# Own halves of the circular and of the last convolution ahead of the waits for their halo rows, and twelve unread matmuls between the halves of the last image

## The chip, the cores and the metric

The kernel runs on one core of one Trainium2 chip. The metric is the device time of one execution in microseconds (us), as the median of several runs; lower is better.

## What is computed

The input `x` is a batch of 8 images of 16 channels and 64 x 64 pixels in f32. Four blocks follow each other, each of them `x = x + conv(group_norm(x))`:

```python
x = x + _L0_conv_ref(_gn(x), L0_conv_W, L0_conv_b)      # a 4 x 4 lattice of 3x3 convolutions
x = x + _L1_conv_ref(_gn(x), L1_conv_weight)            # a circular 3x3 convolution
x = x + _L2_conv_ref(_gn(x), L2_conv_base_weight, L2_conv_spline_weight, L2_conv_spline_scaler, L2_conv_bias_weight)
x = x + _L3_conv_ref(_gn(x), L3_conv_combinator, L3_conv_bias)   # a 3x3 convolution with bias
```

`_gn` normalises each image over 8 groups of 2 channels and all pixels. The second block is written in the reference with FFTs and amounts to a 3x3 convolution with circular borders. The third expands each pixel into 8 spline functions and a SiLU and convolves these 9 features. The fourth is a plain 3x3 convolution with zero borders plus a bias.

## The kernel before, in words

Each engine has a program of its own, written out by hand in the order in which it runs; semaphores (`wait_ge`, `then_inc`) tie the programs together. An engine runs its instructions strictly in that order, so a wait holds up everything behind it. PE is TensorE, DVE VectorE, ACT ScalarE, POOL GpSimd, SP the engine that issues most transfers.

An f32 operand is split into a high and a low part (ACT writes the high part, DVE subtracts it and writes the low one), and each f32 product is three matmuls (`PRODUCTS`, in `products`, L1741 at the matmul): high by high, high by low, low by high. Pixels lie in SBUF with 128 rows: 4 rows of the image by 2 column parities by 16 channels. An output row at the edge of such a group of four needs rows of a neighbouring group. These are the halo rows: SP copies them with four transfers from the tile of own rows to a second tile, once the low part is written.

- The lattice (L1772) runs as 16 cells by 8 images. In its last cell, `k == NC - 1`, PE also runs the circular convolution of image `b - 4` after cell image `b` (`l1_step`). Images 4 to 7 of the circular convolution follow when the cells are over: `l1_step(B - 4)`, `l1_step(B - 3)`, the 2-column matmul `group_means(1, 3)` for the statistics of the next block (L1679), 24 unread matmuls (`keep_warm`, L1809), `l1_step(B - 2)`, `group_means(1, 4)`, 4 unread matmuls, `l1_step(B - 1)`.
- `l1_step(j)` waits for `l1_lo` (DVE has written the low part, L1495), for `l1_halo` (four transfers of SP, L805, `l1_halos`), and for `added[1]` (DVE has read the result bank of image `j - 2`, L1500), and then runs 12 matmuls in `single_step`: 6 on the own tile `F1_OWN`, 6 on the halo tile `F1_HALO`, all into one bank.
- The third block is called KAN here. Its features come from a chain of DVE (L1596, L1602, L1609, L1589) and ACT (L1216, L1227, L1230, L1243) in two groups per image; per image PE runs 24 matmuls for group 0, the halo steps of the image before, 6 for the SiLU, 12 for `l3_step(b - 3)` and 24 for group 1.
- `l3_step(b)`, the last convolution, waits for `l3_lo` (DVE L1566), `l3_halo` (four transfers of SP, L844, `l3_halos`) and `out_staged` (DVE has emptied the bank of image `b - 2`, L1577), and runs `single_step` on 12 matmuls. Images 0 to 4 lie inside the loop; behind the loop stand `group_means(2, 6)`, the halo steps of image 7, `l3_step(5)`, `group_means(2, 7)`, `l3_step(6)`, `l3_step(7)`.
- Behind each `l3_step` DVE adds bias and residual into `OT` (`last_update`, L1577, two instructions) and `OT` is stored with four transfers: for images 5 to 7 two by POOL (L1111) and two by SP (L869). Before `last_update(7)` writes its half of `OT`, it waits for the stores of image 5 on both queues. SP's program has `l3_halos(7)` ahead of the stores of images 5, 6 and 7.

Of the kernel before, what the change touches and what calls it, by code (L numbers as in the profile page):

```python
# [11 lines left out]
B = 8  # L12
# [39 lines left out]
SLOTS_1 = 3  # L52
# [106 lines left out]
def build(nc, x, l0w, l0b, l1w, l2base, l2spline, l2scale, l2bias, l3w, l3bias, consts, out):  # L159
# [80 lines left out]
    with ctx:  # L240
        def sb(name, shape, dt=F32):
            return ctx.enter_context(nc.sbuf_tensor(name, shape, dt))

        def sem(name):
            return ctx.enter_context(nc.semaphore(name))
# [6 lines left out]
        W3 = sb("W3", [P, 2, 4, P], F32R)  # L252
# [35 lines left out]
        W1 = WX[:, 0:8 * P].rearrange("p (a t m) -> p a t m", a=2, m=P)  # L288
# [9 lines left out]
        F1_OWN, F1_HALO = F1[:, :, :, RW:RW + TS], F1[:, :, :, EXT:EXT + TS]  # L298
# [19 lines left out]
        def wide(a):  # L318

            return a.rearrange("p (y w) -> p y w", w=RW)  # L320

        def pixels(a):

            return a.rearrange("p (y w) -> p y w", w=RX)
# [13 lines left out]
        def l3_slot(b):  # L338

            return L3S[max(0, b - B + 3)]  # L340

        PB = [ctx.enter_context(nc.psum_tensor(f"PB{i}", [P, 512], F32)) for i in range(8)]
        OUT_BANK = PB[0:2]
        SPLINE_BANK = (PB[5], PB[6], PB[0])
        RING_BANK = PB[3:7]
        LAST_BANK = PB[3:5]
# [54 lines left out]
        l1_ns, l1_hi, l1_lo, l1_done = sem("l1_ns"), sem("l1_hi"), sem("l1_lo"), sem("l1_done")  # L401
        l1_halo = [sem(f"l1_halo{z}") for z in range(SLOTS_1)]
        l3_ns, l3_hi, l3_lo, l3_done = sem("l3_ns"), sem("l3_hi"), sem("l3_lo"), sem("l3_done")
        l3_halo = [sem(f"l3_halo{z}") for z in range(3)]
# [1264 lines left out]
        def _(pe):  # L1669
# [67 lines left out]
            def products(bank, todo, open_, close):  # L1737

                todo = [(weights[wp], moving[fp]) for weights, moving in todo for wp, fp in PRODUCTS]
                for n, (weights, moving) in enumerate(todo):  # L1740
                    last = nc.tensor.matmul(pixels(bank[:, :]), weights, moving,  # L1741
                                            start=open_ and n == 0, stop=close and n == len(todo) - 1)
                return last

            def at_shift(tile, rows, dx):

                return [wide(tile[0:rows, part])[:, :, dx:dx + RX] for part in range(2)]
# [26 lines left out]
                                                    start=j == 0, stop=j == len(todo) - 1)  # L1774
                        last.then_inc(out_done, 1)

            def single_step(bank, weights, own, halo):

                todo = [((weights[:, 0, 1 - dx], weights[:, 1, 1 - dx]), at_shift(own, P, dx)) for dx in range(2)]
                products(bank, todo, True, False)  # L1780
                todo = [((weights[:, 0, 3 - dx], weights[:, 1, 3 - dx]), at_shift(halo, P, dx))
                        for dx in range(2)]
                return products(bank, todo, False, True)

            def l1_step(j):

                z = j % SLOTS_1
                pe.wait_ge(l1_lo, j + 1)
                pe.wait_ge(l1_halo[z], 4 * 16 * (j // SLOTS_1 + 1))
                if j >= 2:  # L1790
                    pe.wait_ge(added[1], j - 1)
                single_step(OUT_BANK[j % 2], W1, F1_OWN[:, z], F1_HALO[:, z]).then_inc(l1_done, 1)

            turn("cell0")
            pe.wait_ge(mv_ready, 1)
# [10 lines left out]
            def keep_warm(bank, n):  # L1806

                for i in range(n):
                    nc.tensor.matmul(bank[:, :], W3[:, 0, 0], W3[:, 0].rearrange("p t m -> p (t m)"),  # L1809
                                     start=True, stop=True)  # L1810

            keep_warm(PB[2], 8)
            for s in range(STEPS):
                k, b = divmod(s, B)
                if b == 0 and k in (1, 5):
                    keep_warm(PB[2], 10 if k == 1 else 18)
                cell_step(s)
                if (k, b) in TURN_STEPS:
                    turn(TURN_STEPS[k, b])
                if k == NC - 1:  # L1820
                    if b == 0:
                        pe.wait_ge(w1_loaded, dma_total(single_spread(W1)))
                        pe.wait_ge(bias_ready, 1)
                    if b >= 1:
                        group_means(0, b - 1)
                    if b >= 5:
                        group_means(1, b - 5)
                    if b == 4:
                        keep_warm(PB[1], 10)
                    if b >= 4:  # L1830
                        l1_step(b - 4)
            group_means(0, B - 1)
            l1_step(B - 4)
            pe.wait_ge(evac_done, TOTCH)
            pe.wait_ge(w3_loaded, dma_total(single_spread(W3)))
            l1_step(B - 3)
            group_means(1, 3)
            keep_warm(PB[3], 24)
# [18 lines left out]
            def l3_step(b):  # L1857

                z = max(0, b - B + 3)
                pe.wait_ge(l3_lo, b + 1)  # L1860
                pe.wait_ge(l3_halo[z], 4 * 16 * (b + 1 if z == 0 else 1))
                if b >= 2:
                    pe.wait_ge(out_staged, b - 1)
                single_step(LAST_BANK[b % 2], W3, l3_slot(b)[:, 0], l3_slot(b)[:, 1]).then_inc(l3_done, 1)

            def halo_steps(b, g):

# [9 lines left out]
            for b in range(B):  # L1877
                bank = SPLINE_BANK[b % 3]
# [6 lines left out]
                for g in range(KAN_SETS):  # L1885
                    pe.wait_ge(feat_hi, KAN_SETS * b + g + 1)
                    pe.wait_ge(feat_lo, KAN_SETS * b + g + 1)
                    todo = [(own_weights(t, dx), at_shift(feature(t), P, dx))
                            for t in range(GROUP * g, GROUP * (g + 1)) for dx in range(2)]
                    products(bank, todo, g == 0, False).then_inc(tile_used, 1)  # L1890
                    if g == 0:
                        if b < 2:
                            group_means(1, (5, 7)[b])
                        if b == 1:
                            pe.wait_ge(edge_done, 2)
                        if b:
                            halo_steps(b - 1, 0)
                            halo_steps(b - 1, 1)
                        pe.wait_ge(silu_hi, b + 1)
                        pe.wait_ge(silu_lo, b + 1)  # L1900
                        todo = [(own_weights(BASES, dx), at_shift(feature(BASES), P, dx)) for dx in range(2)]
                        products(bank, todo, False, False).then_inc(tile_used, 1)
                        if b >= 3:
                            l3_step(b - 3)
# [4 lines left out]
            halo_steps(B - 1, 0)  # L1909
            halo_steps(B - 1, 1)  # L1910
            l3_step(B - 3)
            group_means(2, B - 1)
            l3_step(B - 2)
            l3_step(B - 1)

# [58 lines left out]
```

## Time and profile before

| | |
|---|---|
| median of 3 runs | 1261.64 us |
| the three runs | 1259.15, 1261.64, 1265.6 us |
| the profiled execution's own time | 1263.95 us |
| its span, first to last instruction | 1262.1 us |
| PE busy | 1177.1 us (93%) |
| DVE busy | 762.3 us (60%) |
| ACT busy | 676.3 us (54%) |
| mean granted TensorE clock | 0.982 |

The profiled execution is a fourth one. Its own time is 1.85 us above its span. Busy time is summed over the whole span; what an engine holds up has to be read from the stretch in question. The granted clock is the share of full speed that TensorE was given: 1.00 is 2.4 GHz, 0.50 is 1.2 GHz.

### The profile page before, as it was taken

To read this page: it belongs to the slowest core of one execution; us is meant where nothing else is said; L and a number is where in the kernel's file an instruction comes from. 1 tells how busy PE (TensorE), PEld (TensorE's weight loads), DVE (VectorE), ACT (ScalarE), POOL (GpSimd) and SP (SyncE) were. 2 spreads that over 40 slices of the span, in tenths; PEclk is the share of its full clock that TensorE was granted. 3 is DMA by queue.
4 is the path that set the end of the run, shared out by engine and by line. 5 is a ranking of instruction groups with operands and counts; after the bars stand their busy time and mean duration, and the time that the engine had idled before them with its cause. 6 is when DMAs were issued, how large, how long until landed. Compare 5 with 4: busy or idle time off the path is not lost.

```text
span 1262.1 us, 14781 instructions
## 1 busy us (share of the span) xinstructions
PE 1177.1 (93%) x5052; PEld 871.8 (69%) x5052; DVE 762.3 (60%) x967; ACT 676.3 (54%) x737; POOL 379.3 (30%) x553
## 2 busy tenths in 40 slices
PE   2988989989999999989999999998999987999995
PEld 1655667666666677766666677777777766777773
DVE  6898962456555522245655552236655789899952
ACT  2677854345445434445445444344444799789821
POOL 8231333424422012412122303634134442104212
PEclk9999999999999999999999999999999998999998
DMA  6899999999999968999999988978799414777873
GB/s 172 230 249 243 289 265 248 183 173 209 209 194 198 218 187 217 218 185 206 201 210 202 197 213 213 256 204 224 193 206 196 59 32 69 108 115 108 126 124 58
DMA packets 103342, 233.65 MB, mean 185 GB/s; under 512 B 35476, under 2 KB 48356, under 8 KB 94884
## 3 DMA queue, kind: packets, MB, share of 16 engines
q1 hardware_dynamic: 80768, 179.28, 65.6%
q0 software_dynamic: 16064, 24.70, 10.8%
q10 hardware_dynamic: 6436, 28.74, 7.3%
q8 instruction: 40, 0.66, 0.2%
q14 instruction: 34, 0.28, 0.1%
HBM read 123.59 MB, written 85.19 MB: 165 GB/s over the span
## 4 chain that ended last, share of the span: by engine, by line
PE 56%; SPq 17%; DVE 12%; DMA 5%; issue 5%; ACT 3%; POOL 2%; DVEq 0%; ACTq 0%; POOLq 0%
PE PB L1772 48%; SPq L830 14%; PE PB L1741 7%; DMA S<-lattice 2%; DVE F L1472 2%; DVE F L1484 2%; DMA F<-F 2%; DVE S L1609 1%; DVE S L1596 1%; DVE S L1602 1%; ACT F L1167 1%; DVE F L1589 1%; SPq L812 1%; SPq L861 1%; ACT F L1243 1%
## 5 line engine op out<-in xcount | busy, mean ns | idle before, releaser
L1772 PE MATMUL PB<-F,WA 128*96 128x512 f32 (+1 forms) x3792 | 917.8, 403 | 27.5 <-ACT S L1178 11.1
L1772 PEld LDWEIGHTS PB<-F,WA 128*96 128x96 f32 (+1 forms) x3792 | 662.7, 176 | 274.0 <-issue 18.8
L1178 ACT ACTIVATE S<-PB,BIAS 96x512 f32<-96x512 f32 (+1 forms) x320 | 211.6, 683 | 305.0 <-PE PB L1772 303.3
L1167 ACT ACTIVATE F<-S 128x2116 fp32r<-128x2116 f32 (+4 forms) x160 | 261.6, 1635 | 184.3 <-issue 67.5
L1472 DVE TENSOR_TENSOR F<-S,F 128x1089 fp32r<-128x1089 f32 (+2 forms) x80 | 121.4, 1518 | 171.0 <-ACT F L1167 170.0
L1474 DVE TENSOR_TENSOR F<-S,F 128x1058 fp32r<-128x1058 f32 x64 | 80.7, 1261 | 189.8 <-ACT F L1167 189.4
L1484 DVE CAST F<-F 64x528 fp32r<-64x528 f32 (+4 forms) x304 | 182.0, 648 | 3.5
L929 POOL DMA_DIRECT2D WA<-taps x76 | 57.0, 751 | 346.9 <-ACT S L1178 310.2
L1741 PE MATMUL PB<-F,WA 128*128 128x512 f32 x576 | 146.7, 412 | 13.9 <-DVE F L1589 13.9
L1741 PEld LDWEIGHTS PB<-F,WA 128*128 128x128 f32 x576 | 112.0, 196 | 42.9 <-issue 14.6
L1475 DVE TENSOR_TENSOR F<-S,F 64x1058 fp32r<-64x1058 f32 x64 | 79.8, 1247 | 0.0
L921 POOL DMA_DIRECT2D taps<-WX x112 | 68.8, 660 | 16.8 <-ACT S L1178 12.6
L896 POOL TENSOR_TENSOR RS<-VE,NHALF 128x1 f32<-128x1 f32 x25 | 27.5, 1099 | 119.2 <-DVE VE L1380 119.1
L914 POOL MEMSET WX<- 48x1600 f32 x18 | 25.8, 1435 | 110.5 <-ACT S L1178 98.7
L1478 DVE TENSOR_TENSOR F<-S,F 128x1089 fp32r<-128x1089 f32 x16 | 20.7, 1295 | 43.7 <-ACT F L1167 43.7
L1243 ACT ACTIVATE F<-S 128x2112 fp32r<-128x2112 f32 x16 | 31.4, 1965 | 22.4 <-DVE S L1609 12.1
L1216 ACT ACTIVATE S<-KS,CB 128x528 f32<-128x528 f32 x64 | 41.8, 724 | 0.2
L1150 ACT ACTIVATE KAN<-X,NBI,RS 64x512 f32<-64x512 f32 (+1 forms) x48 | 32.4, 676 | 15.7 <-POOL F L1121 8.5
L1589 DVE SCALAR_TENSOR_TENSOR F<-S,F 128x1056 fp32r<-128x1056 f32 x32 | 38.8, 1253 | 3.3 <-ACT F L1243 3.3
L1111 POOL DMA_DIRECT2D out<-OT x26 | 14.8, 575 | 82.8 <-DVE OT L1577 82.8
L1596 DVE SCALAR_TENSOR_TENSOR S<-S 128x2112 f32<-128x2112 f32 x16 | 37.7, 2354 | 2.2 <-ACT S L1227 2.2
L1609 DVE SCALAR_TENSOR_TENSOR S<-S 128x2112 f32<-128x2112 f32 x16 | 37.7, 2355 | 0.1
(134 smaller groups left out, 715.9 us busy)
## 6 DMA issues: line engine op xcount, KB each, us to landing
S<-lattice SPq DMA_DIRECT2D x448, 66.1 KB, 4.8
lattice<-S SPq DMA_DIRECT2D x32, 817.5 KB, 6.2
S<-lattice SPq DMA_DIRECT2D x158, 136.1 KB, 3.5
S<-lattice SPq DMA_DIRECT2D x72, 272.5 KB, 4.9
lattice<-S ACTq DMA_DIRECT2D x50, 272.5 KB, 4.8
lattice<-S ACTq DMA_DIRECT2D x16, 817.5 KB, 6.8
lattice<-S SPq DMA_DIRECT2D x48, 272.5 KB, 4.1
S<-lattice SPq DMA_DIRECT2D x158, 70.1 KB, 3.5
```

The source lines that it names most:

```text
L830: sp.dma_start(dst, src).then_inc(image_loaded[q], 16)
L921: pool.dma_start(dst, src).then_inc(tp_stored, 16)
L929: pool.dma_start(dst, src).then_inc(w_loaded[k % 2], 16)
L1167: act.activation(piece_view(s, h, 0), raw_view(s, h), ACT.Copy).then_inc(hi_ready, 1)
L1178: act.activation(wide(to[:, at:at + TS])[:, :, 0:RX], pixels(RING_BANK[n % SLOTS_O][0:cell.rows, :]), ACT.Relu, bias=BIAS[0:cell.rows, k:k ...
L1472: last = nc.vector.tensor_tensor(lo, raw, hi, ALU.subtract)
L1474: nc.vector.tensor_tensor(lo[:, 0:2], raw[:, 0:2], hi[:, 0:2], ALU.subtract)
L1475: last = nc.vector.tensor_tensor(lo[0:4 * C, 2:4], raw[0:4 * C, 2:4], hi[0:4 * C, 2:4], ALU.subtract)
L1484: last = nc.vector.tensor_copy(FP[4 * C:P, slot, part, to:to + n], FP[0:4 * C, slot, 0, source:source + n])
L1589: last = nc.vector.scalar_tensor_tensor(to[:, odd, :, 1], full[:, odd], 0.0, to[:, odd, :, 0].bitcast(F32), ALU.max, ALU.subtract)
L1741: last = nc.tensor.matmul(pixels(bank[:, :]), weights, moving, start=open_ and n == 0, stop=close and n == len(todo) - 1)
L1772: last = nc.tensor.matmul(bank, WA[0:rows, first:first + cell.rows], wide(FZ[0:rows, i % SLOTS_F, base:base + TS])[:, :, 0:RX], start=j == ...
```

## The change

`single_step` is taken apart into `own_part` (6 matmuls on the own tile, which open the sum in the bank) and `halo_part` (6 matmuls on the halo tile, which close it). In `l1_step` and in `l3_step` the wait for the halo transfers moves from ahead of all 12 matmuls to between the two parts. For the last image alone, 12 unread matmuls of 512 columns into bank 5 stand ahead of that wait. No other engine's program changes.

```diff
-            def single_step(bank, weights, own, halo):
+            def own_part(bank, weights, own):
 
                 todo = [((weights[:, 0, 1 - dx], weights[:, 1, 1 - dx]), at_shift(own, P, dx)) for dx in range(2)]
                 products(bank, todo, True, False)
+
+            def halo_part(bank, weights, halo):
+
                 todo = [((weights[:, 0, 3 - dx], weights[:, 1, 3 - dx]), at_shift(halo, P, dx))
                         for dx in range(2)]
                 return products(bank, todo, False, True)
...
                 pe.wait_ge(l1_lo, j + 1)
-                pe.wait_ge(l1_halo[z], 4 * 16 * (j // SLOTS_1 + 1))
                 if j >= 2:
                     pe.wait_ge(added[1], j - 1)
-                single_step(OUT_BANK[j % 2], W1, F1_OWN[:, z], F1_HALO[:, z]).then_inc(l1_done, 1)
+                own_part(OUT_BANK[j % 2], W1, F1_OWN[:, z])
+                pe.wait_ge(l1_halo[z], 4 * 16 * (j // SLOTS_1 + 1))
+                halo_part(OUT_BANK[j % 2], W1, F1_HALO[:, z]).then_inc(l1_done, 1)
...
                 pe.wait_ge(l3_lo, b + 1)
-                pe.wait_ge(l3_halo[z], 4 * 16 * (b + 1 if z == 0 else 1))
                 if b >= 2:
                     pe.wait_ge(out_staged, b - 1)
-                single_step(LAST_BANK[b % 2], W3, l3_slot(b)[:, 0], l3_slot(b)[:, 1]).then_inc(l3_done, 1)
+                own_part(LAST_BANK[b % 2], W3, l3_slot(b)[:, 0])
+                if b == B - 1:
+                    keep_warm(PB[5], 12)
+                pe.wait_ge(l3_halo[z], 4 * 16 * (b + 1 if z == 0 else 1))
+                halo_part(LAST_BANK[b % 2], W3, l3_slot(b)[:, 1]).then_inc(l3_done, 1)
```

On PE, in the circular convolution of images 5 and 6, the order changes like this (`l1_halo2` and `l1_halo0` are the halo semaphores of the two images, `F` and `WX` the pixels and the weights):

```order
-L1741 MATMUL PB<-F,WX 128x512 [waits l1_halo2,l1_lo,added1,w3_loaded,evac_done]
-L1741 MATMUL PB<-F,WX 128x512 x11
...
+L1741 MATMUL PB<-F,WX 128x512 [waits l1_lo,added1,w3_loaded,evac_done]
+L1741 MATMUL PB<-F,WX 128x512 x5
+L1741 MATMUL PB<-F,WX 128x512 [waits l1_halo2]
+L1741 MATMUL PB<-F,WX 128x512 x5
+L1679 MATMUL PB<-MV,TAP_TILE 128x2 [waits mv_ready,turned_lo,nv_ready]
```

No matmul changes its place; the wait for the halo semaphore stands six matmuls later.

On PE, at the end of the program, with the last two images of the last convolution:

```order
-L1741 MATMUL PB<-F,W 128x512 [waits out_staged,l3_halo1,l3_lo]
-L1741 MATMUL PB<-F,W 128x512 x11
-L1741 MATMUL PB<-F,W 128x512 [waits out_staged,l3_halo2,l3_lo]
-L1741 MATMUL PB<-F,W 128x512 x11
...
+L1741 MATMUL PB<-F,W 128x512 [waits out_staged,l3_lo]
+L1741 MATMUL PB<-F,W 128x512 x5
+L1741 MATMUL PB<-F,W 128x512 [waits l3_halo1]
+L1741 MATMUL PB<-F,W 128x512 x5
+L1741 MATMUL PB<-F,W 128x512 [waits out_staged,l3_lo]
+L1741 MATMUL PB<-F,W 128x512 x5
+L1813 MATMUL PB<-W 128x512 x12
+L1741 MATMUL PB<-F,W 128x512 [waits l3_halo2]
+L1741 MATMUL PB<-F,W 128x512 x5
```

Here too the halo waits stand behind six matmuls, and for image 7 behind twelve more (L1813 is the line of `keep_warm` in the changed kernel).

## Rows read from the trace of the kernel before

**Rows 1.** The chain that ended last, by engine.
```profile
PE 56%; SPq 17%; DVE 12%; DMA 5%; issue 5%; ACT 3%; POOL 2%; DVEq 0%; ACTq 0%; POOLq 0%
```
**Rows 2.** Timeline of PE: start us, us, engine, line, operation [idle before <-releaser].
```profile
982.83 2.54 PE L1809 MATMUL PB<-W 128*128 128x512 f32 x10
985.87 3.08 PE L1741 MATMUL PB<-F,WX 128*128 128x512 f32 x12 [0.51 <-DMA F<-F]
...
1012.03 3.08 PE L1741 MATMUL PB<-F,WX 128*128 128x512 f32 x12
1018.02 4.39 PE L1741 MATMUL PB<-F,WX 128*128 128x512 f32 x12 [2.90 <-DMA F<-F]
...
1022.39 5.71 PE L1809 MATMUL PB<-W 128*128 128x512 f32 x24
1027.94 3.01 PE L1741 MATMUL PB<-F,WX 128*128 128x512 f32 x12
```
**Rows 3.** The chain in order of time, circular convolution of image 5.
```profile
1012.86 0.63 DVE F L1495
...
1015.41 2.36 DMA F<-F
1017.77 0.24 issue
1018.02 4.39 PE PB L1741 x12
```
**Rows 4.** Timeline of PE, the next blocks' first waits for features.
```profile
1032.61 3.10 PE L1741 MATMUL PB<-F,WX 128*128 128x512 f32 x12 [0.52 <-issue]
...
1050.55 7.96 PE L1741 MATMUL PB<-F,WA 128*128 128x512 f32 x24 [7.46 <-DVE F L1589]
```
**Rows 5.** Timeline of DVE and ACT between the two blocks.
```profile
1020.53 0.70 DVE L1495 TENSOR_TENSOR F<-KAN,F 128x528 fp32r<-128x528 f32 x1
1022.64 0.16 DVE L1374 TENSOR_SCALAR GM<-PB 128x2 f32<-128x2 f32 x1 [1.41 <-PE PB L1679]
1023.11 2.36 DVE L1609 SCALAR_TENSOR_TENSOR S<-S 128x2112 f32<-128x2112 f32 x1
...
1033.98 2.36 DVE L1596 SCALAR_TENSOR_TENSOR S<-S 128x2112 f32<-128x2112 f32 x1 [1.01 <-ACT S L1227]
...
1008.54 0.69 ACT L1178 ACTIVATE S<-PB,BIAS 128x512 f32<-128x512 f32 x1 [1.14 <-PE PB L1772]
...
1025.50 1.98 ACT L1243 ACTIVATE F<-S 128x2112 fp32r<-128x2112 f32 x1 [2.57 <-DVE S L1609]
```
**Rows 6.** Timeline of PE, start of the last image's features.
```profile
1205.14 10.24 PE L1741 MATMUL PB<-F,WA 128*128 128x512 f32 x42 [0.46 <-DVE F L1589]
```
**Rows 7.** Timeline of PE, the last two images of the last convolution.
```profile
1238.38 0.28 PE L1679 MATMUL PB<-MV,TAP_TILE 128*128 128x2 f32 x2
1239.17 3.08 PE L1741 MATMUL PB<-F,W 128*128 128x512 f32 x12 [0.52 <-issue]
1248.46 5.14 PE L1741 MATMUL PB<-F,W 128*128 128x512 f32 x12 [6.21 <-issue]
```
**Rows 8.** Timeline of DVE and SP at the end.
```profile
1242.61 0.71 DVE L1566 TENSOR_TENSOR F<-KAN,F 128x528 fp32r<-128x528 f32 x1 [1.86 <-ACT F L1255]
1253.63 1.51 DVE L1577 SCALAR_TENSOR_TENSOR OT<-PB,OB,X 64x512 f32<-64x512 f32 x2 [8.77 <-PE PB L1741]
...
1243.35 2.49 SPq L844 DMA_DIRECT2D F<-F  x4
...
1246.72 1.92 SPq L869 DMA_DIRECT2D out<-OT  x3
```
**Rows 9.** Issues of L869 in the whole run, us from issue to landing.
```profile
DMA to landing us min/median/max: 2.5/2.7/4.0
```
**Rows 10.** Granted clock by stretch: from:to us, length, PE busy (x), PEclk, DMA share, GB/s.
```profile
1017.50:1018.00 0.50, 0.00 (x0) 0.54 0.00 0
1018.00:1020.50 2.50, 2.48 (x6) 0.50 0.00 0
...
1246.50:1247.00 0.50, 0.00 (x0) 0.50 1.64 139
1252.50:1253.00 0.50, 0.50 (x3) 0.50 0.00 0
...
68.90:72.90 4.00, 3.92 (x17) 1.00 1.04 246
```
**Rows 11.** Timeline of PE, the idle time ahead of the stretch at 68.90.
```profile
68.98 9.65 PE L1772 MATMUL PB<-F,WA 128*96 128x512 f32 x40 [1.81 <-ACT S L1178]
```

## The prediction

> **What bounds the kernel now.** I read the chain that ended last first: TensorE (PE) has 56% of it, the transfers' queue 17% and DVE 12% [rows 1]. A change on PE can thus pay, but only where PE ends last. The change moves only waits for halo rows, so I went next to the PE timeline and looked for L1741 rows with idle time ahead of them that a transfer ends. In the circular convolution there are two, 0.51 us ahead of image 0 and 2.90 us ahead of image 5 [rows 2]; image 7 has another 0.52 us [rows 4]. In the last convolution there are two, both named "issue": 0.52 us ahead of image 6 and 6.21 us ahead of image 7 [rows 7]. The rows of SP tell what the last one is: L844, four halo transfers, starts at 1243.35 right behind DVE's low part L1566, which ends at 1242.61 + 0.71 = 1243.32 [rows 8]. The remaining steps of both convolutions, 11 of 16, stand behind other PE work and have no such idle time; for them the moved wait costs and gives nothing.
>
> The second view is the granted clock. At 1017.50 it falls from 1.00 to 0.50, after 2.4 us of the 2.90 us of idle time, and stays at 0.50 (1.2 GHz) in the first matmuls of image 5; in the long wait of image 7 it is at 0.50 by 1246.50 and still there at 1253.00 [rows 10]. So image 5 takes 4.39 us and image 7 5.14 us for 12 matmuls, where image 4 and image 6 take 3.08 us at 2.4 GHz [rows 2, 7].
>
> **Price of a half step.** At the full clock 12 matmuls are 3.08 us, or 0.257 each; half a step is 1.54 us, and about 1.65 with the drain of its last matmul, which is an estimate: 6 start-to-start gaps are shorter than 3.08/2. At the half clock it is 5.14/2 = 2.57 us [rows 7].
>
> **Circular convolution, image 0.** The ten unread matmuls end at 982.83 + 2.54 = 985.37, and the step starts at 985.87 [rows 2]. The own half fills 1.5 us from 985.37 on and the halo rows are there by 985.87, so the step ends 0.50 us earlier. PE then has work without a pause until ACT waits for it, 1.14 us ahead of L1178 at 1008.54 [rows 5]; ACT feeds DVE's low part, and DVE releases SP's transfers. All of them move by **0.50 us**.
>
> **Circular convolution, image 5.** L1495 ends, the fourth transfer lands at 1017.77, PE starts at 1018.02 [rows 3]. Image 4's step ends near 1012.03 + 3.08 = 1015.1. Now the own half runs from 1015.1 to 1016.6, the halo half from 1018.0 to 1019.65 (all still 0.50 less, by the step before), against 1018.02 + 4.39 = 1022.41: PE is 2.8 us ahead, and 3.3 with image 0's part. Who takes that? DVE waits 1.41 us for the statistics matmul L1679 behind this step, until 1022.64 [rows 5]; DVE's work before it, L1495, ends at 1020.53 + 0.70 = 1021.23. With the matmul in at about 1019.8 this wait goes, but for some 0.05 us, and DVE's own chain is next late. So L1609 at 1023.11 comes 1.36 us sooner, ACT L1243 behind it, which waited 2.57 us for L1609, comes with it, and so does DVE L1596 at 1033.98, which waits for ACT [rows 5]. The other 1.4 us of PE end in idle time: PE waits 7.46 us for DVE L1589 at 1050.55 [rows 4]. This edit is worth **1.36 us**. Even at the half clock the halo half would end at 1018.0 + 2.57 = 1020.6, ahead of 1021.23; the value is safe from below as long as the clock had fallen before. In a run in which it had not, the old step ended at 1018.02 + 3.08 = 1021.1 and the edit is worth nothing. So its bounds are 0 and 1.4 us.
>
> **Image 7 of the circular convolution** would start its own half earlier, too, but behind it PE only gets to the 7.46 us of waiting sooner: nothing.
>
> **From there to the end.** The feature loop is DVE and ACT work with PE close behind; the last image's features start with 0.46 us of waiting for DVE L1589 [rows 6]. A shift of both engines by 1.86 us goes through. Images 0 to 4 of the last convolution have no wait for a transfer: nothing.
>
> **Last convolution, image 6.** Its own half starts behind L1679 at 1238.66 instead of at 1239.17 [rows 7], so PE is done 0.5 us sooner, near 1241.8. Nobody is released by it: the low part of image 7 hangs on L1679, POOL and ACT [rows 8]. Worth nothing.
>
> **Last convolution, image 7.** From 1243.35 on, the own half and the 12 unread matmuls: 18 x 0.257 = 4.6 us at the full clock, to 1248.0. The halo rows are there at 1248.46, so the unread matmuls do not delay them, with 0.5 us to spare. The halo half ends at 1248.46 + 1.65 = 1250.1 instead of 1253.60: **3.5 us**. The clock has to hold for that. PE now idles from 1241.8 to 1243.35, 1.55 us, and then 0.5 us. The nearest row is the 1.81 us of idle time ahead of 68.98, behind which the clock stayed at 1.00 [rows 11, 10]; the 2.4 us of image 5 are the nearest after which it fell. I take the full clock. Next late are the stores of image 5, for which DVE waits ahead of the last L1577: SP's second one is issued at 1246.72 [rows 8] and lands 2.7 us later in the median, 4.0 at most [rows 9], so at 1249.4, at most 1250.7. That is just ahead of 1250.1.
>
> The lower bound of this edit comes from the clock too. In the profiled execution all 12 matmuls ran at the half clock, the dearest case; in another run of the old kernel the clock may come back within the step, at best giving 3.08 us and leaving a gain of 1.5 us. Here the Trainium skill bears on the reading ("TensorE: Matmul & The Clock Gate", section "What's actually happening"): the point at which the clock changes is not tied to the kernel and differs between runs. The three runs, 6.45 us apart, would fit that; one trace cannot show it.
>
> For the price of a matmul the rows and a page differ. The rows give 0.238 us for each of 24 unread ones [rows 2]. The Trainium skill ("TensorE: Matmul & The Clock Gate", section "Back-to-back issue gap") has about 131 ns for a matmul of 512 columns in a stream with weight loads. By its figure, as an estimate, 18 of them would end near 1245.7, and with 2.7 us of idle time the halo half would run at the half clock, for a gain of 2.6 us instead of 3.5. The trace does not agree, and the sum goes by the rows.
>
> **The sum** against the profiled execution: 1263.95 - 0.50 - 1.36 - 3.5 = 1258.6 us. That execution lies 2.3 us above the median of the three runs and had the half clock wherever the edits act, so the median run has less to win. I take 0.9 us off the two terms that hang on the clock, between no deduction and the 3.4 us that both bounds together allow: 5.36 - 0.9 = 4.5, and 1261.64 - 4.5 = **1257.1 us**. Between 3.0 and 6.4 us of gain the forecast's own range is 1255.2 to 1258.6.
>
> **Rivals.**
> 1. *The circular convolution's gain is swallowed.* DVE's wait of 1.41 us vanishes but another in its chain grows, the clock had not fallen in most runs, or the loop gives it back. For it: DVE and ACT wait on each other all through the loop. Only the end and a little more is won: 3.3 us, 1258.3 us.
> 2. *More arrives than summed.* PE leaves image 5's step 3.3 us sooner. Should the loop be tied to PE rather than to DVE, all of that comes through: 3.3 + 3.5 = 6.8, 1254.8 us. Against it stand the 7.46 us that PE waits for DVE [rows 4]; for it, that PE has only 0.46 us of slack at the last image [rows 6].
> 3. *The unread matmuls stand in the way* (slower). If the clock falls in the 1.55 us of idle time, 18 matmuls take 18 x 0.428 = 7.7 us, to 1251.05, though the halo rows are in at 1248.46, and the halo half ends at 1253.6. That equals the dearest old case and is up to 2.06 us worse than the cheapest. It decides from 0.284 us per matmul on (5.11/18). With nothing but image 0's 0.5 us on the other side: 1262.3 us. Rows 11 speak against.
> 4. *The stores of image 5 end last.* DVE starts at 1250.7 instead of 1250.1: 1257.7 us.
> 5. *Nothing reaches the end*, because the waits named "issue" have another cause than the halo rows: 1261.6 us. Against it: the fourth transfer's landing and PE's start lie together for image 5 [rows 3].
> 6. *The short matmul*, by the mechanism above (2.7 us idle, half clock in the last half step): 0.9 us less, 1258.0 us.
>
> **How the numbers follow.** Chances: forecast 0.50, rival 1 0.17, rival 2 0.16, rival 3 0.06, rival 4 0.05, rival 5 0.05, rival 6 0.01. Faster or slower count from 0.5% on, 6.3 us, about what a measurement of this kernel can tell; that line is at 1255.3 and 1267.9. Faster: most of rival 2 (0.13) and a fifth of the forecast's range (0.10), 0.23. Slower: 0.02, only by scatter on top of rival 3. The range from 1253.3 to 1261.0 leaves out the far ends of rivals 2, 3 and 5.
>
> **What would show it.** Right: in the trace after, 6 matmuls of image 5 near 1014.6 and 6 near 1017.5; DVE's L1374 behind them with next to no wait; the granted clock at 1.00 from 1243 to the end of the last matmul; L1577 about 1.65 us behind the landing of the last halo transfer. Wrong: a clock of 0.50 at the unread matmuls, a wait of L1577 for a store, or DVE's wait turning up again further on in the feature loop.

## The result, and the profile after

| | before | after |
|---|---|---|
| median of 7 runs | 1261.64 us | 1255.14 us |
| lowest to highest | 1259.15 to 1265.6 us | 1251.75 to 1257.64 us |
| profiled execution, own time | 1263.95 us | 1253.46 us |
| its span | 1262.1 us | 1251.6 us |

The ratio after to before is 0.9949, with a 95% interval of 0.9931 to 0.9967: 6.5 us less in the median, 4.2 to 8.7 us by the interval. One run of the kernel before (1298.72 us) and one without the unread matmuls (1323.43 us) in the experiments below ran at a mean granted clock of 0.85 and 0.82 and are left out of every ratio. The two profiled executions differ by 10.5 us, which is more than the interval allows and has to be taken apart first.

PE around the circular convolution of images 0 and 5 in the changed kernel (timeline; it answers to [rows 2]):

```profile
979.07 2.54 PE L1813 MATMUL PB<-W 128*128 128x512 f32 x10
981.45 3.01 PE L1741 MATMUL PB<-F,WX 128*128 128x512 f32 x12
...
1007.53 4.52 PE L1741 MATMUL PB<-F,WX 128*128 128x512 f32 x18
1013.31 1.70 PE L1741 MATMUL PB<-F,WX 128*128 128x512 f32 x6 [1.26 <-DMA F<-F]
```

Two things are to be seen. The ten unread matmuls, whose code and everything ahead of them is unchanged, start at 979.07 instead of 982.83: 3.76 us of the 10.5 come from before the first changed instruction. And the 18 matmuls at 1007.53 are image 4's step and the own half of image 5 in one piece; the wait for the halo rows is down from 2.90 to 1.26 us and the halo half runs at full clock, 1.70 us for 6.

DVE behind it (timeline; [rows 5] had 1.41 us of waiting ahead of L1374):

```profile
1016.04 0.70 DVE L1495 TENSOR_TENSOR F<-KAN,F 128x528 fp32r<-128x528 f32 x1
1016.65 0.15 DVE L1374 TENSOR_SCALAR GM<-PB 128x2 f32<-128x2 f32 x1
...
1017.12 2.36 DVE L1609 SCALAR_TENSOR_TENSOR S<-S 128x2112 f32<-128x2112 f32 x1
```

The wait is gone; L1495 starts 4.49 us earlier than before, L1609 5.99 us earlier, so 1.50 us were won here.

PE and DVE at the end (timelines; [rows 7, 8]):

```profile
1230.48 0.28 PE L1679 MATMUL PB<-MV,TAP_TILE 128*128 128x2 f32 x2
1230.62 3.11 PE L1741 MATMUL PB<-F,W 128*128 128x512 f32 x12
1235.48 2.73 PE L1741 MATMUL PB<-F,W 128*128 128x512 f32 x6 [1.74 <-DVE F L1566]
1238.01 3.45 PE L1813 MATMUL PB<-W 128*128 128x512 f32 x12
1241.30 1.59 PE L1741 MATMUL PB<-F,W 128*128 128x512 f32 x6
...
1234.72 0.71 DVE L1566 TENSOR_TENSOR F<-KAN,F 128x528 fp32r<-128x528 f32 x1 [1.85 <-ACT F L1255]
1242.93 1.51 DVE L1577 SCALAR_TENSOR_TENSOR OT<-PB,OB,X 64x512 f32<-64x512 f32 x2 [5.96 <-PE PB L1741]
```

The granted clock in this stretch (by windows; columns as in [rows 10]):

```profile
1234.00:1235.00 1.00, 0.00 (x0) 1.00 0.71 74
1236.00:1238.50 2.50, 2.50 (x8) 0.50 0.45 74
1239.50:1241.00 1.50, 1.50 (x8) 1.00 0.78 179
```

The own half starts right behind the low part, as forecast, but takes 2.73 us: after 1.74 us of idle time the clock fell to 0.50, 0.3 us into the own half by windows of 0.25 us. The unread matmuls end later for it, and the halo half starts at 1241.30 without a pause ahead of it, 5.87 us behind the low part, where the old one had started 5.14 us behind it. From the end of L1566 to the start of L1577 it is 1242.93 - 1235.43 = 7.50 us instead of 10.31.

### The profile page after: what moved, and what is told of

Read it like the earlier page. It is cut to its first block, busy times and chain, and to the rows that moved or that the text cites. A ratio compares the mean times of both kernels' runs of the same rounds, so it can differ in the third digit from the quotient of the medians.

```text
span 1251.6 us, 14801 instructions
## 1 busy us (share of the span) xinstructions
PE 1176.7 (94%) x5064; PEld 871.9 (70%) x5064; DVE 763.8 (61%) x967; ACT 677.0 (54%) x737; POOL 386.9 (31%) x553
## 4 chain that ended last, share of the span: by engine, by line
PE 65%; DVE 12%; SPq 10%; issue 4%; DMA 3%; ACT 3%; POOL 2%; ACTq 0%; DVEq 0%; POOLq 0%
PE PB L1772 57%; SPq L830 8%; PE PB L1741 6%; DVE S L1596 2%; DMA S<-lattice 2%; DVE F L1472 2%; DVE S L1609 2%; DVE S L1602 2%; DVE F L1589 1%; DVE F L1484 1%; DMA F<-F 1%; SPq L861 1%; ACT F L1167 1%; PE PB L1813 1%; SPq L812 1%
## 5 line engine op out<-in xcount | busy, mean ns | idle before, releaser
L1741 PE MATMUL PB<-F,WA 128*128 128x512 f32 x576 | 144.6, 408 | 15.2 <-DVE F L1589 14.1
L1243 ACT ACTIVATE F<-S 128x2112 fp32r<-128x2112 f32 x16 | 31.4, 1963 | 20.7 <-DVE S L1609 10.5
L1589 DVE SCALAR_TENSOR_TENSOR F<-S,F 128x1056 fp32r<-128x1056 f32 x32 | 38.8, 1253 | 3.1 <-ACT F L1243 3.1
L1609 DVE SCALAR_TENSOR_TENSOR S<-S 128x2112 f32<-128x2112 f32 x16 | 37.7, 2354 | 0.1
```

The costliest lines, as they stand in the source:

```text
L1609: nc.vector.scalar_tensor_tensor(U2[n % 2], A2[n % 2], 4.0, U2[n % 2], ALU.add, ALU.min)\
```

## One ruler for all profiles

The scatter between executions is larger than any of the edits, so each profile is cut at events that all kernels share. T0 is the start of the ten unread matmuls ahead of image 0's circular step; T1 is PE's start behind its first long wait for features ([rows 4], 1050.55); T2 is the end of the last L1566; T3 is the start of the last L1577. Each value is the difference of two starts or ends in rows like those above. "Half clock" is the time in which the granted clock was 0.50 in that stretch, summed over windows of 0.25 us.

| profile | T0 | T0-T1 | T1-T2 | half clock in it | T2-T3 | T3-end |
|---|---|---|---|---|---|---|
| before | 982.83 | 67.72 | 192.77 | 11.4 | 10.31 | 8.47 |
| before, once more | 984.74 | 68.58 | 191.11 | 6.6 | 10.45 | 8.62 |
| image 0 only | 977.79 | 65.61 | 192.98 | 12.1 | 10.54 | 8.58 |
| image 5 only | 977.04 | 67.31 | 191.12 | 6.5 | 10.45 | 8.58 |
| circular only | 972.41 | 65.50 | 191.23 | 6.9 | 10.55 | 8.71 |
| last only | 977.52 | 67.07 | 193.34 | 12.9 | 7.51 | 8.56 |
| after | 979.07 | 65.49 | 190.87 | 6.9 | 7.50 | 8.67 |
| after, once more | 980.43 | 65.47 | 193.85 | 14.2 | 7.56 | 8.59 |
| no unread | 988.24 | 65.48 | 192.94 | 11.8 | 7.00 | 8.54 |
| no unread, once more | 979.56 | 65.47 | 194.43 | 14.1 | 8.07 | 8.57 |
| 24 unread | 981.03 | 65.50 | 194.32 | 14.4 | 10.28 | 8.57 |
| gap filled | 982.63 | 65.47 | 191.37 | 6.5 | 6.83 | 8.50 |
| two queues | 979.86 | 65.50 | 192.37 | 10.8 | 5.71 | 8.56 |
| loop filled | 975.04 | 65.48 | 189.62 | 0.0 | 5.71 | 8.55 |

T0 spreads over nearly 16 us (972.41 to 988.24) though all that lies ahead of it is the same program. The two profiles of before and after differ by 3.76 us there, by 2.23 in T0-T1, by 1.90 in T1-T2 and by 2.81 in T2-T3; the end is 0.20 longer. That is the 10.5 us. Only T0-T1 and T2-T3 hold changed waits that something waited for; the 3.76 and 1.90 us lie where the scatter of unchanged code is larger than that.

## Experiments

### The two edits apart

The circular convolution alone (the last one goes back to its old order):

```diff
-                own_part(LAST_BANK[b % 2], W3, l3_slot(b)[:, 0])
-                if b == B - 1:
-                    keep_warm(PB[5], 12)
                 pe.wait_ge(l3_halo[z], 4 * 16 * (b + 1 if z == 0 else 1))
+                own_part(LAST_BANK[b % 2], W3, l3_slot(b)[:, 0])
```

The last convolution alone (the circular one goes back to its old order):

```diff
-                own_part(OUT_BANK[j % 2], W1, F1_OWN[:, z])
                 pe.wait_ge(l1_halo[z], 4 * 16 * (j // SLOTS_1 + 1))
+                own_part(OUT_BANK[j % 2], W1, F1_OWN[:, z])
```

> Only the circular convolution has its halves apart; the last convolution waits for its halo rows ahead of all 12 matmuls and has no unread ones. Theory (the edits act where they stand, 0.5 us at image 0 and up to 1.4 us at image 5, and DVE's chain passes it on): no idle time of PE ahead of image 0's step, DVE L1374 behind image 5's step waits under 0.2 us instead of 1.41, and the end is as before: about 10.3 us from the end of the last low part (L1566) to the start of the last L1577. Median 0.5 to 2 us below before. Rival (most of the 6.5 us of the median comes from here, because PE passes on its whole 3.3 us): 3.5 us or more below before. Rival (none arrives): within 0.5 us.

> Only the last convolution is changed, own half ahead of the halo wait and 12 unread matmuls for image 7; the circular one is as before. Theory: from the end of the last L1566 to the start of the last L1577 6.8 us where the clock holds and 7.5 to 8.3 us where it falls in the idle time ahead, against 10.3 us; DVE L1374 behind image 5's circular step waits up to 1.4 us as before. Median 2 to 3.5 us below before. Rival (the end is worth nothing beyond noise, the gain is in the circular step): within 1 us of before.

Circular only: median 1258.02 us against 1260.27, ratio 0.9981 (0.9954 to 1.0008). T0-T1 is 65.50 and T2-T3 10.55: the circular edit does all of its work in the first stretch and none at the end. Last only: median 1255.99 us, ratio 0.9972 (0.9947 to 0.9997), T2-T3 7.51 and T0-T1 67.07. In its profile the old circular step of image 5 is to be seen again, in PE's and DVE's timelines:

```profile
1011.87 4.48 PE L1741 MATMUL PB<-F,WX 128*128 128x512 f32 x12 [2.79 <-DMA F<-F]
...
1016.67 0.16 DVE L1374 TENSOR_SCALAR GM<-PB 128x2 f32<-128x2 f32 x1 [1.47 <-PE PB L1679]
```

Both medians lie a little beyond what was expected: 2.25 us less for the circular edit alone (expected 0.5 to 2), 4.28 for the last one alone (expected 2 to 3.5).

So the two gains stand side by side and add up. The rival that all of it comes from the circular step, with PE's 3.3 us passed on, falls: T0-T1 never gets under 65.47 us in any kernel. By their ratios the two are 2.4 and 3.5 us, with intervals about as wide as the gains; the ruler is what prices them.

### Images 0 and 5 of the circular convolution apart

The order is the new one for image 0 alone; the other kernel has 5 in place of 0:

```diff
+                if j != 0:
+                    pe.wait_ge(l1_halo[z], 4 * 16 * (j // SLOTS_1 + 1))
                 own_part(OUT_BANK[j % 2], W1, F1_OWN[:, z])
-                pe.wait_ge(l1_halo[z], 4 * 16 * (j // SLOTS_1 + 1))
+                if not (j != 0):
+                    pe.wait_ge(l1_halo[z], 4 * 16 * (j // SLOTS_1 + 1))
```

The last convolution is as before in both.

> The kernel before, with the circular halves apart for image 0 alone. Theory (image 0's part moves PE, ACT and DVE by some 0.6 us, image 5's does the rest): from the start of the ten unread matmuls to PE's start behind its 7 us wait for features 67.0 us, against 67.72 before, 65.48 in the changed kernel and 67.07 where the circular convolution was left alone. DVE's wait ahead of L1374 behind image 5's step stays near 1.4 us. Rival (image 0 gives nothing that lasts): 67.7 us.

> The kernel before, with the circular halves apart for image 5 alone. Theory (DVE's 1.4 us wait behind image 5's step is what this edit removes, and no more of PE's 3.3 us): 66.0 to 66.3 us on the same stretch, DVE's wait ahead of L1374 gone, and PE's wait for features as much longer as PE is early. Rival (PE passes all on): 64.5 us or less.

> The kernel before once more, for a second profile. Theory: L1566 to L1577 10.2 to 10.6 us with the clock at 0.50 in the last step; from the ten unread matmuls to PE's start behind the wait for features 67.0 to 67.8 us; the ten unread matmuls themselves start anywhere from 972 to 988 us, since what differs between executions lies in the lattice. Rival (the profile before was an odd one at the end): under 9.5 us.

One run each: 1257.27, 1256.33 and, for the kernel before, 1265.29 us. The ends are as expected, T2-T3 10.45 to 10.54 us. The first stretch came out otherwise in all three. Image 0 only has 65.61 us, almost all of the gain, because the old step of image 5 cost nothing in this execution. Its PE timeline and its clock there:

```profile
1012.16 3.10 PE L1741 MATMUL PB<-F,WX 128*128 128x512 f32 x12 [2.77 <-DMA F<-F]
```

```profile
1012.00:1015.00 3.00, 2.84 (x12) 1.00 0.00 0
```

It waits for the halo rows as long as ever, 2.77 us, but the clock did not fall, the 12 matmuls take 3.10 us, and DVE does not wait. The kernel before, once more, has the opposite (PE, then DVE):

```profile
1019.63 5.46 PE L1741 MATMUL PB<-F,WX 128*128 128x512 f32 x12 [2.92 <-DMA F<-F]
...
1025.42 0.16 DVE L1374 TENSOR_SCALAR GM<-PB 128x2 f32<-128x2 f32 x1 [2.58 <-PE PB L1679]
```

All 12 matmuls ran at the half clock, and DVE waited 2.58 us. Image 5 only gives 67.31 us, more than expected, because the step of image 0, unchanged in it, waited longer for its halo rows:

```profile
981.16 3.08 PE L1741 MATMUL PB<-F,WX 128*128 128x512 f32 x12 [1.58 <-DMA F<-F]
```

Neither old wait has a fixed price. Against the 65.48 us of the changed code, image 5's old step cost about 1.5, 2.7, 1.6 and 0.1 us in the four profiles that have it, and image 0's about 0.7, 0.4, 0 and 1.8 us: the first is DVE's wait ahead of L1374 and the hand-over, the second what is then left of T0-T1. Two readings of the traces support this split. The wait ahead of L1374 was 1.41, 2.58, 1.47 and 0 us. Image 0's step started 3.04, 2.68, 2.38 and 4.12 us behind T0 (985.87 - 982.83 in [rows 2], 981.16 - 977.04 in the row above), against 2.38 us in the changed kernel; that is 0.7, 0.3, 0 and 1.7 us more. The average is 1.5 and 0.7, together 2.2 us, and the changed code is always at the floor: 65.47 to 65.50 in nine profiles. The edit takes out a cost and its scatter. The expected start of the ten unread matmuls, 972 to 988 us, held.

### The unread matmuls of image 7

Three variants of the changed kernel. Without them:

```diff
-                if b == B - 1:
-                    keep_warm(PB[5], 12)
```

With 24:

```diff
-                    keep_warm(PB[5], 12)
+                    keep_warm(PB[5], 24)
```

With 6 more ahead of the wait for the low part ("gap filled"):

```diff
+                if b == B - 1:
+                    keep_warm(PB[5], 6)
                 pe.wait_ge(l3_lo, b + 1)
```

> The changed kernel without the 12 unread matmuls, so that behind image 7's own half PE idles some 3.5 us until the halo rows are in. Theory (the unread matmuls keep or bring back the clock): the halo half runs at the half clock, 2.6 us instead of 1.6, starting when the rows land, 5.1 us behind the low part; L1566 to L1577 takes 7.8 us. Rival (they stand in the way as often as they help): 7.5 us or less, the same as in the changed kernel or shorter, and the median is within 1 us of the changed kernel's.

> The changed kernel without its 12 unread matmuls once more. Theory (where the clock stands at the end is a matter of when it is looked at): L1566 to L1577 comes out anywhere from 6.8 to 7.9 us, the latter if the clock is at 0.50 in the halo half. Rival (PE's own half alone keeps the clock): 7.0 us again, the clock at 1.00 up to the halo half.

> The changed kernel once more, unedited, for a second look at its end and a second set of times. Theory (the clock falls in image 7's idle time in some executions and not in others): L1566 to L1577 takes 6.8 us if the clock holds and up to 8.3 us if it falls; the way from the ten unread matmuls of the circular convolution to the end is 272 to 273 us as before, and what differs between executions lies ahead of it, in the lattice. Rival (the changed kernel always loses 0.7 us at the end): 7.5 us again, within 0.1.

> 24 unread matmuls in place of 12 between image 7's halves. Theory (they stand ahead of the halo half on PE and delay it once they outlast the transfers): own half and 24 unread take 1.5 + 24 x 0.238 = 7.2 us at the full clock, 2.1 us beyond the landing at 5.1, so L1566 to L1577 takes 8.8 to 9.0 us, and 9.5 or more if the clock falls first; median 1.5 to 3 us above the changed kernel. Rival (the transfers or the stores bound the end, not PE): 7.5 us as before.

> The changed kernel with 6 more unread matmuls between the step of image 6 and the wait for the low part of image 7, to fill the 1.74 us in which PE idles there. Theory (the clock fell in the changed kernel's profile because of this idle time): the clock stays at 1.00 to the last matmul, L1566 to L1577 takes 6.8 us, 0.7 below the changed kernel's profile. Rival (the clock falls anyway, or the 18 matmuls are too long even at full clock): 7.5 us or more.

The changed kernel once more: T2-T3 7.56 us, after 7.50 and, in last only, 7.51. The theory that this varies from 6.8 to 8.3 fell in these three profiles; the rival, always 0.7 us lost, held. The rows say why it comes out alike: the half clock began 0.3, 0.4 and 1.2 us into the own half (after, last only, after once more), lasted about as long in each, and was over before the halo half. The changed kernel once more, PE and its clock:

```profile
1239.81 2.02 PE L1741 MATMUL PB<-F,W 128*128 128x512 f32 x6 [1.77 <-DVE F L1566]
1241.62 4.23 PE L1813 MATMUL PB<-W 128*128 128x512 f32 x12
1245.69 1.58 PE L1741 MATMUL PB<-F,W 128*128 128x512 f32 x6
```

```profile
1240.00:1241.00 1.00, 1.00 (x5) 1.00 0.00 0
1241.25:1244.25 3.00, 3.00 (x9) 0.50 0.74 111
1244.50:1247.00 2.50, 2.50 (x12) 1.00 0.51 94
```

Here the half clock took more of the unread ones (4.23 us for 3.45) and less of the own half (2.02 for 2.73); the sum is the same. Median 1254.54 us, ratio 0.9948 (0.9922 to 0.9973).

Without unread matmuls T2-T3 was 7.00 us in one profile and 8.07 in the other. The first, PE:

```profile
1246.71 1.71 PE L1741 MATMUL PB<-F,W 128*128 128x512 f32 x6 [1.74 <-DVE F L1566]
1251.82 1.79 PE L1741 MATMUL PB<-F,W 128*128 128x512 f32 x6 [3.40 <-DMA F<-F]
```

The second, PE and its clock:

```profile
1239.52 2.55 PE L1741 MATMUL PB<-F,W 128*128 128x512 f32 x6 [1.77 <-DVE F L1566]
1244.56 2.93 PE L1741 MATMUL PB<-F,W 128*128 128x512 f32 x6 [2.50 <-DMA F<-F]
```

```profile
1244.00:1246.00 2.00, 1.44 (x3) 0.50 0.64 120
```

The same code: once the clock holds until near the end of the halo half, which starts when the rows land, and once it is at 0.50 for all of it. The first profile met the rival (7.5 us or less), the second lies 0.2 us above the 7.9 us that the theory allowed. The average, 7.5 us, is that of the kernel with 12 unread matmuls. The medians agree: in the set of runs that has both, 1254.32 us without them and 1254.54 with them; the other pair, from different sets, is 1256.16 and 1255.14. The ratios are 0.9969 and 0.9946 without, 0.9949 and 0.9948 with them, each good to some 0.3%. So nothing shows that the 12 unread matmuls, where the change puts them, earn anything. In the four profiles with unread matmuls behind a fall (12 or 24 of them) the clock was back at 1.00 for the halo half, and behind the one fall without them it was not; but 12 stand 0.7 us too long ahead of it. Whether they bring the clock back, or when it would have come back by itself, these few profiles do not show.

With 24 of them T2-T3 is 10.28 us. PE's rows:

```profile
1240.90 2.23 PE L1741 MATMUL PB<-F,W 128*128 128x512 f32 x6 [1.75 <-DVE F L1566]
1242.93 6.74 PE L1813 MATMUL PB<-W 128*128 128x512 f32 x24
1249.50 1.59 PE L1741 MATMUL PB<-F,W 128*128 128x512 f32 x6
```

Twelve more cost 2.75 us at the end; the expectation had 9.5 us or more for the case that the clock falls first, which it did. Median 1259.45 us, ratio 0.9978 (0.9953 to 1.0003), 4.9 us above the changed kernel's in the same set of runs, where 1.5 to 3 had been expected and the end accounts for 2.75; the rest is no more than these medians scatter. PE, and not the stores, bounds the end.

With the gap filled the clock stays at 1.00 and PE waits for the halo rows once more:

```profile
1237.61 1.55 PE L1813 MATMUL PB<-W 128*128 128x512 f32 x6
1239.52 1.69 PE L1741 MATMUL PB<-F,W 128*128 128x512 f32 x6 [0.36 <-DVE F L1566]
1241.04 2.90 PE L1813 MATMUL PB<-W 128*128 128x512 f32 x12
1244.57 1.69 PE L1741 MATMUL PB<-F,W 128*128 128x512 f32 x6 [0.63 <-DMA F<-F]
```

T2-T3 is 6.83 us, the forecast's own figure for a clock that holds (1.65 + 5.1). Median 1254.49 us, ratio 0.9955 (0.9926 to 0.9985); the 0.7 us are under what the medians can tell. It was the 1.74 us of idle time ahead that lost them: the three profiles with this gap filled (this one and the two of the next sections) have the clock at 1.00 from there to the last matmul, and each of the six with the gap open has a fall on the way.

### The halo transfers of image 7 on two queues

The gap-filled kernel is the base; its 6 unread matmuls ahead of the low part's wait stay.

```diff
-                for dst, src in image_halos(slot[:, 0], slot[:, 1]):
+                for dst, src in list(image_halos(slot[:, 0], slot[:, 1]))[0:2 if b == B - 1 else 4]:
...
+            act.wait_ge(l3_lo, B)
+            slot = l3_slot(B - 1)
+            for dst, src in list(image_halos(slot[:, 0], slot[:, 1]))[2:4]:
+                act.dma_start(dst, src).then_inc(l3_halo[2], 16)
...
-                    keep_warm(PB[5], 12)
+                    keep_warm(PB[5], 8)
```

> The kernel with 6 unread matmuls ahead of image 7's wait for the low part and 8 (for 12) between its halves, and with two of image 7's four halo transfers issued by ACT, which is idle there, instead of all four by SP. Theory (with the clock held, the issue of four transfers one after the other, 0.63 us each, is what the end waits for): the last one is issued 1.25 us sooner, so L1566 to L1577 takes 5.5 us in place of 6.8, and the median lies about 2 us below the changed kernel's. Rival (the landing is what takes the time, or the stores of image 5 end last): 6.5 us or more.

SP and ACT issue at the same time, and PE starts 3.98 us behind the low part instead of 5.1 (this kernel's lines are 4 higher: L1745 is the convolution):

```profile
1237.76 1.22 SPq L844 DMA_DIRECT2D F<-F  x2
1237.76 1.49 ACTq L1341 DMA_DIRECT2D F<-F  x2
...
1241.71 1.69 PE L1745 MATMUL PB<-F,W 128*128 128x512 f32 x6 [0.40 <-DMA F<-F]
```

T2-T3 is 5.71 us (expected 5.5). Median 1252.63 us against 1261.52, ratio 0.9924 (0.9897 to 0.9951), the median 1.9 us under the changed kernel's in the same set of runs. With the clock held, the issue of one transfer after the other was the next thing that the end waited for.

### The idle times of the feature loop filled

```diff
+                if b in (2, 3):
+                    keep_warm(PB[3], 9)
...
                 for g in range(KAN_SETS):
+                    if b == 0 and g == 1:
+                        keep_warm(PB[3], 26)
```

> The two-queue kernel with unread matmuls in the three idle times of PE in the feature loop: 26 ahead of group 1 of image 0 (7.5 us of waiting), 9 each ahead of group 0 of images 2 and 3 (2.6 us each). Theory (the half clock behind these waits costs about half of the time it lasts, and PE passes it on from image 2 on): the granted clock stays at 1.00 from there to the end, and the stretch from PE's start behind the first wait to the end of the last low part takes 188 to 190 us, against 190.9 to 194.4 us in the profiles so far, with 6.5 to 14.4 us at the half clock. Median 1.5 to 4 us below the two-queue kernel's, which would make it the fastest. Rival (that stretch is bound by DVE): unchanged, 191 us or more.

The clock in all of the loop, and the first of the three places (the kernel of the last section was the base; L1593 is its L1589):

```profile
1040.50:1230.00 189.50, 185.60 (x786) 1.00 0.69 107
```

```profile
1032.87 6.07 PE L1817 MATMUL PB<-W 128*128 128x512 f32 x26
1040.52 5.96 PE L1745 MATMUL PB<-F,WA 128*128 128x512 f32 x24 [1.58 <-DVE F L1593]
```

T1-T2 is 189.62 us, the shortest of all, with no time at the half clock; over the table the stretch grows from there to 194.4 us as the half clock in it grows to 14.4 us, so that about a third of the half-clock time arrives (4.8 of 14.4 us; the expectation had about half). A stretch bound by DVE alone would not have changed with the clock of PE. It is one profile, and the three places were not filled one by one. Median 1251.39 us against 1260.12, ratio 0.9932 (0.9909 to 0.9955). The medians do not separate it from the two-queue kernel, which ran on another chip against other runs; by the ruler, from T0 to the end, it takes 269.36 us against 272.14 there, 272.53 in the changed kernel and 279.27 before. Both beat the kernel before. The expected 1.5 to 4 us below the two-queue kernel are not to be seen in the ratios (0.9932 and 0.9924), and the intervals of both overlap that of the changed kernel; that they are faster than it is shown by the ruler alone.

## Why the prediction was right, and where its sizes were off

**Time and range.** Forecast 1257.1 us (1253.3 to 1261.0), measured 1255.14. The ratio of 0.9949 lies on the line between "same" and "faster", which had 0.75 and 0.23; the interval reaches to both sides of it. By the ruler the edits are worth 2.2 us in T0-T1 and 10.46 - 7.52 = 2.9 us at the end (averages over five old and three new ends), 5.1 us in all. The medians' 6.5 us hold that in their interval, and so do the 6.6 us of the second set. Whether the 1.4 us between them are more than scatter stays open; no stretch of the table shows a further difference between the old code and the new, and T1-T2 is as scattered in both.

**The deduction of 0.9 us** was one of two steps that failed; the other is the full clock at image 7, below. I took the profiled execution for a dear case in which the half clock happened to lie over image 7's step. All five profiles of the old end have it, 10.31 to 10.55 us: after 6 us of idle time it is no accident. At image 5 the deduction was right in kind, since the old step costs from 0.1 to 2.7 us, but the bounds of 0 and 1.4 us were too narrow above, as I had taken one observed wait for the greatest, though a step wholly at the half clock can be read from [rows 7].

That the sum without it, 5.36 us, and the ruler's 5.1 lie so near each other is in part luck: image 7's term was 0.6 us too large and the two circular ones together 0.3 too small. The forecast's 4.5 us lies 0.6 below the ruler and 2.0 below the medians, inside a range that leaves nearly 4 us to each side.

**Image 0**, 0.50 us forecast: 0.7 on average, from 0 to 1.8, by when the halo rows land against the ten unread matmuls. **Image 5**, 1.36 forecast: 1.50 between the two first profiles, 1.5 on average. That DVE takes just its own wait and PE's further lead ends in idle time held. **Image 6 and the steps without a wait**: nothing, as forecast.

**Image 7**, 3.5 us forecast: 2.81 between the profiles, 2.9 on average. The term was mis-sized at "I take the full clock". The nearest row, 1.81 us of idle time without a fall, did not carry over: after 1.74 to 1.77 us the clock fell in five of six profiles with that gap. With it fell "the unread matmuls do not delay them, with 0.5 us to spare": they delayed the halo half by 0.7 us. The prediction had named a clock of 0.50 at the unread matmuls as a sign of being wrong, and it came. This was the mechanism of rival 3, at a fifth of its price (0.7 us for 3.5), as the clock came back before the halo half and not after it. The filled gap shows the forecast's 6.8 us once the clock holds.

**The other rivals.** The circular gain was not swallowed (rival 1), and PE did not pass on its 3.3 us (rival 2): T0-T1 has its floor at 65.47. The stores did not end last (rival 4): in the changed kernel and in all variants the last L1577 waits for PE, even at 5.71 us. Rival 5 falls with T2-T3. Rival 6's price of a matmul fell, too: 24 unread ones took 5.71 us at the full clock here, 0.238 each, not the about 131 ns of the Trainium skill ("TensorE: Matmul & The Clock Gate", section "Back-to-back issue gap").

## What to carry to other kernels

Work that does not need the late operand goes ahead of its wait, and what it is worth is read at the engine that waits behind it, not at the one that starts sooner: PE gained 3.3 us at image 5 and passed on 1.5. Unread matmuls paid here in the idle time behind which the clock had fallen (6.83 us for 7.5); between a wait's start and the useful work they are a delay as soon as they outlast the wait. Where executions scatter by more than an edit, cut the traces at events that both kernels share, and profile the old kernel more than once before a wait's price is taken from it.

## What was not expected of the hardware

- The clock fell behind 1.74 to 1.77 us of idle time in five of six profiles, each time only when PE had been busy again for 0.3 to 1.2 us, but in the variant without unread ones it held over 1.74 and 3.40 us with only 6 matmuls between them, to near the end of the halo half, and over 2.77 us in image 0 only. Idle times of 2.77 and 2.92 us ahead of the same 12 matmuls left DVE without a wait in one execution and with 2.58 us in another.
- The program ahead of T0 is the same in all kernels, and T0 spreads from 972.4 to 988.2 us, while T3 to the end spreads by 0.24 us and T0-T1 in the changed code by 0.03 us.
- Of up to 14.4 us at the half clock in the feature loop, up to 4.8 us arrive at the end of the loop, though PE has idle time in it. Why not all or nothing of it arrives stays open.
